# A mixture-of-experts transformer kernel: the last layer's gathers of five batches copy instead of accumulate, and memsets stand behind the scatters of three batches

## What is computed

```python
x = x + attn_a(layernorm(x));  x = x + ffn(layernorm(x))
x = x + attn_b(layernorm(x));  x = x + ffn(layernorm(x))

def ffn(x):                       # N = 4096 tokens, d = 128
    sel = sigmoid(xf @ expert_sel.T)
    sel_val, sel_idx = top_k(sel, 4)
    h = einsum('nd,kde->nke', xf, keys)
    scores = relu(h) * gates[:, :, None]      # gates: sel_val at sel_idx, 0 elsewhere
    return einsum('nke,kev->nv', scores, values)
```

## Time and profile before

| | us |
|---|---|
| median of 3 runs | 1334.67 (1326.5 to 1334.81) |
| profiled execution | 1321.22 |
| its span | 1319.5 |
| busy in it: PE / DVE / ACT / POOL | 832.7 / 711.2 / 559.9 / 876.3 |

### The profile page before, as it was taken

One profiled execution on the slowest core, in us unless ns is written; L12 is line 12 of the kernel. 1 busy time (PEld: TensorE's weight loads), 2 busy tenths in 40 slices (PEclk: granted clock), 3 DMA queues, 4 the chain that ended last, 5 costly groups with the idle time before them and its releaser, 6 DMA issues.

```text
span 1319.5 us, 22434 instructions
## 1 busy us (share of the span) xinstructions
PE 832.7 (63%) x7290; PEld 611.6 (46%) x7290; DVE 711.2 (54%) x2037; ACT 559.9 (42%) x1505; POOL 876.3 (66%) x860
## 2 busy tenths in 40 slices
PE   1889887887787677978885254524767669900000
PEld 0534444443443267977874243423666669900000
DVE  2878988788783256645667475533555436500000
ACT  1177676766666434744543233121534336500000
POOL 6255577887675743478888878775304338888887
PEclk9699999899897779989987576656978779955555
DMA  6855553232712336888852222123435449943333
GB/s 179 287 204 190 179 172 100 74 103 87 219 56 81 112 92 173 245 196 204 180 100 39 44 45 35 44 44 102 123 105 144 120 126 271 245 67 44 44 43 48
DMA packets 235217, 163.80 MB, mean 124 GB/s; under 512 B 15968, under 2 KB 223840, under 8 KB 235104
## 3 DMA queue, kind: packets, MB, share of 16 engines
q1 hardware_dynamic: 185696, 112.00, 29.6%
q0 software_dynamic: 45056, 33.59, 14.5%
q10 hardware_dynamic: 4352, 16.78, 3.3%
HBM read 78.94 MB, written 83.36 MB: 123 GB/s over the span
## 4 chain that ended last, share of the span: by engine, by line
POOL 31%; PE 25%; issue 13%; DVE 12%; DMA 7%; ACT 5%; another core or an unknown queue 5%; SPq 1%; POOLq 0%; ACTq 0%; DVEq 0%
POOL x_res L1659 23%; DMA x_res<-result_rows,dest 6%; PE ps L630 4%; POOL sorted_rows L1647 4%; PE ps L729 4%; PE ps L738 3%; PE ps L589 3%; ACT arena L930 2%; PE ps L718 2%; SPq L452 1%; PE ps L677 1%; POOL arena L1691 1%; DVE row_max L1155 1%; PE ps L647 1%
## 5 line engine op out<-in xcount | busy, mean ns | idle before, releaser
L1659 POOL DMA_INDIRECT x_res<-result_rows,dest x256 | 397.9, 1554 | 100.2 <-issue 73.9
L930 ACT ACTIVATE arena<-ps 128x512 f32<-128x512 f32 x320 | 183.1, 599 | 83.4 <-PE ps L562 77.9
L1647 POOL DMA_INDIRECT sorted_rows<-v_aug,dest x128 | 124.5, 973 | 123.7 <-DVE dest L1342 55.5
L1647 POOL DMA_INDIRECT sorted_rows<-x_scaled,dest x128 | 127.4, 995 | 75.2 <-ACT x_scaled L896 39.3
L1354 DVE COPY arena<-ps 128x512 f32<-128x512 f32 x128 | 88.1, 689 | 145.6 <-PE ps L718 79.5
L729 PE MATMUL ps<-arena 128*128 128x128 f32 x1024 | 152.2, 297 | 21.3 <-DVE arena L1354 10.0
L738 PE MATMUL ps<-arena 128*128 x1024 | 145.3, 288 | 11.8 <-ACT arena L919 11.5
L919 ACT COPY arena<-ps 128x512 f32<-128x512 f32 x128 | 74.8, 584 | 182.5 <-PE ps L738 119.9
L729 PEld LDWEIGHTS ps<-arena 128*128 128x128 f32 x1024 | 138.4, 210 | 27.0 <-issue 14.4
L589 PE MATMUL ps<-arena 64*128 64x128 bf16 (+3 forms) x576 | 129.6, 304 | 32.0 <-DMA arena<-k_parts 17.9
L1155 DVE TENSOR_REDUCE row_max<-ps 128x1 f32<-128x512 f32 (+1 forms) x192 | 126.9, 681 | 35.0 <-PE ps L609 32.7
(11 more groups left out here) (202 smaller groups left out, 1507.3 us busy)
## 6 DMA issues: line engine op xcount, KB each, us to landing
arena<-sorted_rows SPq DMA_DIRECT2D x128, 256.0 KB
result_rows<-arena SPq DMA_DIRECT2D x128, 256.0 KB
sorted_rows<-arena ACTq DMA_DIRECT2D x16, 1024.0 KB, 4.6
arena<-q_parts SPq DMA_DIRECT2D x16, 512.0 KB
arena<-k_parts SPq DMA_DIRECT2D x16, 512.0 KB
q_parts<-parts SPq DMA_DIRECT2D x52, 128.0 KB, 2.7
k_parts<-parts SPq DMA_DIRECT2D x50, 128.0 KB, 2.9
x_res<-result_rows,dest POOLq DMA_INDIRECT x256
```

Of the source, the lines that this page charges most:

```text
L930: nc.scalar.activation(prob[:, grp % 2, pr % 2, PROB_AT[u]:PROB_AT[u] + T], ps[:, v % 2, :], ACT.Exp, scale=SCALE_A).then_inc(exp_done, 1)
L1647: g.indirect_dma_start(sorted_d[b // HALF][:, :], bass.IndirectOffsetOnAxis(dest[:, 16 * b + n:16 * b + n + 1], 0), scaled_rows(layer, b)[ ...
L1659: g.indirect_dma_start(x[:, TT * b + t, :], None, result_d[layer][b // HALF][:, :], bass.IndirectOffsetOnAxis(dest[:, at:at + 1], 0), comp ...
```

## The change

There are two edits, both in layer 1.

- The gathers of batches 3 to 7 (`PLAIN`) no longer accumulate. They copy the rows into one of three buffers of SBUF that are no longer used (`x_scaled` and the two halves of `v_aug`, in turn), and DVE adds each choice's four tiles onto `x_res` with one 128x512 add, four adds a batch. DVE waits for the landings, POOL for the adds of a buffer's earlier batch, and SP writes the batch out behind its last add. Batches 0 to 2 accumulate as before, and so does all of layer 0.
- Behind each of the 16 scatters of batches 5, 6 and 7 POOL issues a memset of `w_attn` (128x640 fp32, unused by then), which waits for the memset before it.

```diff
+PLAIN = tuple((1, b) for b in range(3, B))
+PACED_FROM = 5
...
+        gather_buffers = (xs_a, xs_b[:, 0], xs_b[:, 1])
+        def gather_buffer(layer, b):
+            return b % 3 if layer else 0
+        def last_reader(layer, b):
+            mine = PLAIN.index((layer, b))
+            earlier = [n for n in range(mine) if gather_buffer(*PLAIN[n]) == gather_buffer(layer, b)]
+            return TOPK * (earlier[-1] + 1) if earlier else 0
...
-                for lane in landed:
-                    sp.wait_ge(lane, landed_count("gather", 1, b))
+                if (1, b) not in PLAIN:
+                    for lane in landed:
+                        sp.wait_ge(lane, landed_count("gather", 1, b))
+                else:
+                    sp.wait_ge(added, TOPK * (PLAIN.index((1, b)) + 1))
...
+            def add_rows(layer, b):
+                xb = x[:, TT * b:TT * b + TT, :]
+                for c in range(TOPK):
+                    for lane in landed:
+                        dve.wait_ge(lane, landed_count("gather", layer, b) - 16 * (TOPK - 1 - c))
+                    if c:
+                        dve.wait_ge(added, TOPK * PLAIN.index((layer, b)) + c)
+                    nc.vector.tensor_tensor(xb, xb, gathered_rows(layer, b)[:, TT * c:TT * c + TT, :], ALU.add).then_inc(added, 1)
...
+            for b in range(B):
+                if (1, b) in PLAIN:
+                    add_rows(1, b)
...
+            def rest():
+                n = next(rests)
+                if n > 1:
+                    pool.wait_ge(rested, n - 1)
+                g.memset(w[:, :], 0.0).then_inc(rested, 1)
...
+                adding = (layer, b) not in PLAIN
+                if not adding and last_reader(layer, b):
+                    pool.wait_ge(added, last_reader(layer, b))
...
+                        if adding:
+                            g.indirect_dma_start(x[:, TT * b + t, :], None, rows, index, compute_op=ALU.add).then_inc(lane, 16)
+                        else:
+                            g.indirect_dma_start(gathered_rows(layer, b)[:, TT * c + t, :], None, rows, index).then_inc(lane, 16)
...
                     for n in range(TT * TOPK):
                         scatter(1, late, n)
+                        if late >= PACED_FROM:
+                            rest()
```

More of the change, by code:

```diff
@@ L376, in build @@
         scaled = sem("scaled")
+        rested = sem("rested")
+        added = sem("added")
         ln2 = sem("ln2")
@@ L398, in scaled_rows, with gathered_rows @@
             return xs_b[:, b % 2] if layer else xs_a
+        gather_buffers = (xs_a, xs_b[:, 0], xs_b[:, 1])
+        def gather_buffer(layer, b):
+            return b % 3 if layer else 0
+        def gathered_rows(layer, b):
+            return gather_buffers[gather_buffer(layer, b)]
+        def last_reader(layer, b):
+            mine = PLAIN.index((layer, b))
+            earlier = [n for n in range(mine) if gather_buffer(*PLAIN[n]) == gather_buffer(layer, b)]
+            return TOPK * (earlier[-1] + 1) if earlier else 0
         def evacuated(name, b):
@@ L1519, in combined_stats @@
             def combined_stats(b):
-                for lane in landed:
-                    dve.wait_ge(lane, landed_count("gather", 0, b))
+                if (0, b) in PLAIN:
+                    add_rows(0, b)
+                    dve.wait_ge(added, TOPK * (PLAIN.index((0, b)) + 1))
+                else:
+                    for lane in landed:
+                        dve.wait_ge(lane, landed_count("gather", 0, b))
                 finish(ln_stats(x[:, TT * b:TT * b + TT, :], st0, mv0, rs0, b, ln2))
@@ L1632, in _ @@
             g.tensor_tensor(maskswap, maskswap, upper, ALU.add).then_inc(swapped, 1)
-            transfers = count()
+            transfers, rests = count(), count(1)
+            def rest():
[3 more added lines that the diff above has]
+                g.memset(w[:, :], 0.0).then_inc(rested, 1)
             def next_lane():
@@ L1658, in gather @@
                         at = 16 * b + TOPK * t + c
-                        g.indirect_dma_start(x[:, TT * b + t, :], None, result_d[layer][b // HALF][:, :],
-                                             bass.IndirectOffsetOnAxis(dest[:, at:at + 1], 0), compute_op=ALU.add).then_inc(lane, 16)
+                        rows, index = result_d[layer][b // HALF][:, :], bass.IndirectOffsetOnAxis(dest[:, at:at + 1], 0)
+                        if adding:
+                            g.indirect_dma_start(x[:, TT * b + t, :], None, rows, index, compute_op=ALU.add).then_inc(lane, 16)
+                        else:
+                            g.indirect_dma_start(gathered_rows(layer, b)[:, TT * c + t, :], None, rows, index).then_inc(lane, 16)
             def norm(b, mv, rs, rstd, dst, done):
```

## The result

| | before | changed |
|---|---|---|
| median, us | 1331.18 (4 runs, 1326.5 to 1334.81) | 1248.42 (4 runs, 1246.62 to 1250.66) |
| ratio | | 0.938 (0.934 to 0.942) |
| profiled execution, its span | 1321.22, 1319.5 | 1247.83, 1239.4 |
| granted clock, mean | 0.806 | 0.821 |

What follows compares the result with a forecast made beforehand. POOL's gathers were taken to bound the tail, with dense scatter bursts holding engines ahead of it. Span 1319.5 - 37.0 (-46.4 + 0.3 + 9.1) - 15.3 = 1267.2; median 1334.67 - 52.3 = 1282.4 us, range 1254 to 1303.

Steps and rivals of the forecast that it cites:

- the copying gather: Layer 1, batches 3 to 7: a gather without add costs POOL 0.96 us like a scatter, not 1.54, pace 1.26.
- the term: Tail of layer 1: 79 intervals between gathers, each 1.26 us instead of 1.847, gain 46.4 us.
- the memset's price and its cover: Scatters of batches 5 to 7: memset 0.65 us, pace 1.78; 48 memsets (31 us) cost nothing, 5.6 us of cover remain.
- the relief: Bursts of batches 5 to 7: time other engines are held that spacing the scatters gives back, between nothing and -37 us.
- full relief: All held time of the scatter bursts given back: layer 1's gathers start at 1039.9 instead of 1076.82, -37 us; chance 0.18.
- A third of it ... -15.3: Scatter bursts: a third of the held time given back, gathers start at 1061.5, -15.3 us; the value the forecast took.
- window of PE beside gathers at 1.85 us: From 1080 us on, beside gathers at 1.85 us each, PE is busy for 69.94 of 70 us.
- the bursts were the whole cause: Rival: spacing the scatters of batches 5 to 7 gives back all held time, -37 us, 1260.7 us; chance 0.18.
- the holds and the last add: Tail: DVE adds lengthening POOL's gathers, +9.1 us, and the final add ahead of SP's write, +0.3 us.
- the step to the median: From span to median time: the median stands 13.5 us above the profiled execution's 1321.22, and that distance is kept.
- +9.1: Tail of layer 1: nineteen DVE adds beside gathers each hold POOL 0.48 us, +9.1 us; bounds 0 and 12.9.
- half of the collisions spared: Low end of the range, 1254: half of the +9.1 us for DVE adds holding POOL's gathers doesn't occur.

Runs made afterwards that it cites:

- second measurement: The changed kernel unaltered, measured again in six runs beside eleven of the kernel before: 1252.62 us (1241.1 to 1256.33), ratio 0.940.
- half the rows: Changed kernel without memsets, each scatter of batches 5 to 7 carrying 64 of its 128 rows (output not right): one run, 1287.7 us.
- copies only: Changed kernel without any memsets, gathers of batches 3 to 7 still copying: 1288.4 us, ratio 0.967.
- half of each row: Changed kernel without memsets, scatters of batches 5 to 7 writing only 64 channels of each row to their own buffer (output not right): 1281.4 us, ratio 0.971.
- tiny memsets: Changed kernel with memsets of 8 elements instead of 640 behind the scatters of batches 5 to 7: 1288.31 us, ratio 0.964.
- mid memsets: Changed kernel with memsets of 192 elements instead of 640 behind the scatters of batches 5 to 7: 1281.66 us, ratio 0.962.
- landing pace: Changed kernel without memsets; POOL instead waits behind each scatter of batches 5 to 7 until it has landed: 1288.64 us, ratio 0.969.

## Why the prediction was right or wrong

**Right: the copying gather.** It takes 0.94 us at a pace of 1.25, forecast 0.96 and 1.26. Choosing the scatter as the nearest row, on the ground that only the accumulation makes a transfer dearer for POOL, was sound. From the first gather of layer 1 on the gain is 46.4 us, the term to the digit, but that is luck: the 79 intervals gave 47.0, and the 48 gathers ahead of them cost 0.7 more than before. POOL's own work still sets the pace of the tail, and the landings, 2.65 us after the start where 2.84 was forecast, stay clear of `FLIGHT`.

**Right: the memset's price and its cover.** 0.65 us, a pace of 1.78, and 28.4 us for a burst. But the cover held only while batch 7's scatters ended ahead of the stores, and the relief itself took that away: they now gate both the gathers and the loads, 9 us behind the stores' end, as the forecast had worked out for full relief. Trimming the last memsets moved the time by less than can be told.

**Wrong: "A third of it ... -15.3", with "I take the third".** This step has most of the error: the mechanism was named, its size was not worked out. The trace gave 33.7 us, against the -37 that the forecast had for all of it; the first gather starts at 1043.10, where full relief gave 1039.9 and the third gave 1061.5. The two possible causes were named right: pace or direction. The choice between them was a middle value with nothing behind it, and full relief got a chance of 0.18 only. The forecast's own window of PE beside gathers at 1.85 us was the stronger evidence, and it spoke for the pace. The runs of shorter memsets settle it: the pace decides, at 1.27 nothing is relieved, at 1.41 a part, at 1.78 all. The direction doesn't matter. The rival "the bursts were the whole cause" was right in mechanism, and with its 1260.7 still 12.3 us too slow: 9.4 for the holds and the last add, 6.2 for the step to the median, less the 3.3 by which the relief fell short of 37.

**Wrong: "+9.1" for adds that hold POOL.** The measured cost is 0, the lower bound. The step scaled the length by which a gather is held with the overlap (0.88 of it) and let a transfer under way be held. One case in the trace of before could not show that it is the start of a transfer that is held. By the rows since, a gather that starts into a 1.22 us operation waits nearly all that is left of it, and one that has begun does not wait at all.

**Wrong by a little, and partly open: the step from span to median.** The spans differ by 80.1 us where 52.3 was forecast: 18.4 for the relief, 9.4 for the holds and the last add (which cost nothing, not 0.3). The forecast kept the 13.5 us between the median and the profiled execution; here 0.6 are left. That the changed kernel's executions agree better is not shown, since its four runs lie within 4 us and the six of the second measurement within 15; the profile fell near the median. Against that, the time outside the span has risen from 1.7 us to 8.4. It is 1.7 to 2.4 in every run of the kernel before whose span is on record, 1.8 to 2.2 where only the memsets were put in, and 5.7 to 8.5 in all kernels with copying gathers but the one with more DVE work behind the adds, which has 2.0. Its cause wasn't found. Together: 1267.2 + 15.2 was forecast, 1239.4 + 9.0 measured.

**The chances.** Faster by over 1% had 0.91, and so it was. The range was too narrow at its low end because it let full relief come with only half of the collisions spared. Both at their better end give 1334.67 - 46.4 - 37.0 = 1251.3. The collisions were at theirs (none) and the relief nearly (33.7 of 37).

**What the profile was to show:** scatters every 1.78 us and memsets of 0.65, yes. Some 19 gathers longer by 0.3 to 0.7, none. 108.6 us for batches 3 to 7, 98.9. Unnamed waits of 24 us ahead of the last stage, none in the bursts. First gather at 1061, it was 1043.

**What stays open** is which resource a dense row takes. Held time by the pace of the transfers in the bursts of batches 5 to 7:

| pace, us | kernel | held | besides, "issue" in pieces of over 2 us |
|---|---|---|---|
| 1.20 | half the rows | 44 us | 7 us |
| 1.26 | before | 35 us | 13 us |
| 1.26 | copies only | 46 us | none |
| 1.26 | half of each row | 35 us | 9 us |
| 1.27 | tiny memsets | 40 us | 10 us |
| 1.41 | mid memsets | 14 us | 15 us |
| 1.78 | changed kernel | none | none |
| 2.5 and more | landing pace | none | 6 us |

It goes with the number of transfers per time, not with what they carry. POOL's busy share isn't it: in the changed kernel's bursts it is busy for 25.5 of 28 us and holds nothing. Nor is it the share that POOL spends on transfers: 1.54 of 1.85 us, 83%, with accumulating gathers, which hold nothing, and 0.96 of 1.41, 68%, with the mid memsets, which hold some. What the traces add is that the late handoffs looked at here are those out of PE, not those out of DVE. That PE's signals are slowed by what POOL writes for each transfer, or by the transfers' own signals, is a guess; no run here separates these, and none has another engine than POOL issue such a row.

## What to carry to other kernels

If engines wait for a releaser that the profile can't name, look for what runs densely beside them, and space it out before making anything faster: in this kernel scatters whose end nothing waited for, made slower by 40%, took 3% off the time, and gathers made faster beside the experts cost 48 us. A spaced row costs nothing as long as its end isn't waited for, so find that end first, and look again after the gain, since it moves the gate. Where a trace leaves two causes open with a factor between them, put the forecast on the one that more rows support, and not in the middle.

## What the hardware showed that was not expected

- Bursts of 16 indirect transfers from POOL every 1.20 to 1.27 us hold PE, DVE and ACT up for 35 to 46 us in three bursts, and an unbroken row of copying gathers every 1.25 us all but stops them (0.47 us of PE work in 20, with the DMA engines at 0.19 of their time). At 1.78 no such wait is left.
- In the places looked at beside such rows, DVE started 4.5 to 11.2 us after PE's modelled end, while PE started 0.06 to 0.15 us after DVE's.
- An indirect transfer of 64 rows takes POOL 0.90 us, one of 128 rows 0.96, with half or full rows; with an accumulate 1.54. The price is for the transfer, and for adding, and hardly for rows.
- In 15 of 16 cases a transfer that started on POOL during a 1.22 us DVE operation of two SBUF inputs ended about 0.82 us behind that operation's end; in the sixteenth, 0.03 us behind DVE's start, DVE took 1.29 and the transfer its 0.94. Transfers that had begun took their usual 0.94.
